# The last two batches of a latent attention: softmax sums taken on all 128 rows and inverted whole, in place of inverted on 32 rows and spread by DMA

## What is computed

```python
# latent attention: 16 heads, each batch has 64 context rows (masked) and 64 latent rows as keys
q  = layer_norm(x) @ Wq
kv = concatenate([layer_norm(ctx), layer_norm(x)], 1) @ Wkv
weight = softmax(where(mask, (q * scale) @ (k * scale).T, -max), axis=-1)   # over 128 keys
x = x + (weight @ v) @ Wout
# then: layer_norm(x); rmsnorm, quantise, @ w1, relu, square, rmsnorm, quantise, @ w2; + x; layer_norm
```

## Time and profile before

| | us |
|---|---|
| median of 3 runs | 1608.52 (1604.91 to 1608.94) |
| the profiled execution, its own time | 1607.23 |
| its span in the trace | 1605.4 |
| PE busy in the span | 1424.4 (89%) |
| DVE busy | 1134.2 (71%) |
| ACT busy | 963.8 (60%) |
| POOL busy | 303.9 (19%) |

### The profile page before, as it was taken

How to read it: one execution, slowest core, us unless ns; L and a number is a source line. 1 busy time by engine, 2 the same in 40 slices (tenths; PEclk the granted TensorE clock), 3 DMA queues, 4 the chain that set the end, 5 groups by cost and what they waited for, 6 DMA issues and landing times. The chain is left out here.

```text
span 1605.4 us, 32269 instructions
## 1 busy us (share of the span) xinstructions
PE 1424.4 (89%) x12643; PEld 868.5 (54%) x12658; DVE 1134.2 (71%) x2363; ACT 963.8 (60%) x1498; POOL 303.9 (19%) x278
## 2 busy tenths in 40 slices
PE   7999999998999788878887868999999999999962
PEld 4666666665664333334333345566666666666541
DVE  4666778885336799889988943445667767766788
ACT  2332367675555988789878944345556665555433
POOL 3434335352001100111010031111112211110101
PEclk9999999997999999999999979999999999999995
DMA  4000000001000000000000002222222222222210
GB/s 178 2 2 2 2 19 12 15 6 54 1 1 1 1 2 1 1 1 1 1 1 4 1 14 53 62 68 65 61 60 60 66 67 68 65 57 57 69 47 17
DMA packets 41013, 50.78 MB, mean 32 GB/s; under 512 B 9248, under 2 KB 23200, under 8 KB 40480
## 3 DMA queue, kind: packets, MB, share of 16 engines
q1 hardware_dynamic: 40576, 48.06, 11.7%
q10 hardware_dynamic: 288, 0.67, 0.1%
HBM read 13.04 MB, written 2.10 MB: 9 GB/s over the span
## 5 line engine op out<-in xcount | busy, mean ns | idle before, releaser
L1836 DVE TENSOR_TENSOR l_px<-psum,l_share 128x1024 f32<-128x1024 f32 x64 | 78.4, 1224 | 154.6 <-PE psum L1552 104.6
L1694 ACT ACTIVATE l_prob<-psum,l_bias 128x1024 f32<-128x1024 f32 x64 | 71.3, 1115 | 172.5 <-PE psum L1529 172.5
L1541 PE MATMUL psum<-l_XT,l_A 128*128 128x256 f32 x512 | 126.3, 391 | 3.3 <-ACT l_XT L1709 3.1
L1524 PE MATMUL psum<-l_th,l_XT 128*128 128x512 f32 x256 | 125.6, 613 | 1.4 <-DVE stream L1843 0.7
L1588 PE MATMUL psum<-l_px,l_N 128*128 128x256 f32 x512 | 124.2, 386 | 1.8 <-ACT l_r L1735 1.8
L1552 PE MATMUL psum<-l_prob,l_X 128*128 128x512 f32 x256 | 122.8, 603 | 0.0
L1817 DVE TENSOR_REDUCE l_top<-psum 128x8 bf16<-128x1024 f32 x64 | 78.2, 1221 | 43.6 <-PE psum L1603 43.5
L895 PE MATMUL psum<-f_projX,f_kT 64*128 64x512 f32 x256 | 77.1, 679 | 34.1 <-DVE f_frac L1266 18.6
L1588 PEld LDWEIGHTS psum<-l_px,l_N 128*128 128x128 f32 x512 | 94.0, 191 | 19.1 <-issue 4.7
L1541 PEld LDWEIGHTS psum<-l_XT,l_A 128*128 128x128 f32 x512 | 93.6, 193 | 15.0 <-ACT l_XT L1709 3.6
L1266 DVE TENSOR_TENSOR f_frac<-psum,f_whole 128x1024 f32<-128x1024 f32 x80 | 98.0, 1225 | 2.7
(11 more groups left out here) (309 smaller groups left out, 3198.9 us busy)
## 6 DMA issues: line engine op xcount, KB each, us to landing
l_share<-l_recip SPq DMA_DIRECT2D x512, 64.0 KB, 2.0
early_weights<-in_weights SPq DMA_DIRECT2D x1, 2405.0 KB, 11.2
c_cs<-in_ctx SPq DMA_DIRECT2D x16, 128.0 KB, 2.1
f_qf<-in_l_mats SPq DMA_DIRECT2D x1, 2048.0 KB, 8.0
out<-l_normed SPq DMA_DIRECT2D x16, 128.0 KB, 2.0
l_craw<-in_ctx SPq DMA_DIRECT2D x15, 128.0 KB, 2.3
late_weights<-in_weights SPq DMA_DIRECT2D x1, 1089.0 KB, 11.2
relbias<-in_relbias ACTq DMA_DIRECT2D x1, 512.0 KB, 5.2
```

What stands on the lines that cost most here:

```text
L1524: nc.tensor.matmul(ps[:, SC + n, :], XT[:, q % 3, k, :, :], th[:, q % 2, k, 8 * n:8 * n + 8, :], start=True, stop=False)
L1541: last = nc.tensor.matmul(ps[:, at + j // 2, (j % 2) * 256:(j % 2 + 1) * 256], A[:, QB * k + j, :], XT[:, q % 3, :, 1, :], start=True, sto ...
L1836: nc.vector.tensor_tensor(px[:, q % 2, :, k, :], ps[:, GA:GA + 2, :].rearrange("p a (h s) -> p (a h) s", s=S), share[:, (b // 2) % 2, b % ...
```

## The change

Only the last pair, p = 31 (batches 62 and 63), is treated otherwise.

- Its `sums`, `invert` and `spread` are gone: one `sums` (L1562 x8), two transposes and a small reciprocal, 16 DMAs.
- PE takes the sums of batch 62 (step 63) and 63 (step 64) with a 128 x 128 matrix of ones (`broad_sums`), so that the 1024 sums of a batch stand on all 128 rows in two banks: `RO` for 62, `SC` for 63.
- DVE inverts these 128 x 1024 sums whole, straight into `share` (`invert_last`): batch 62 at the end of step 63, batch 63 in step 64.
- `gather(63)` writes into `RO`, and waits for the first inversion (which reads `RO`) and no longer for the division of batch 62; it stands ahead of `tokens_turned(13)` now.
- On DVE `divide(62)` and `divide(63)` move to the front of steps 64 and 65, behind `tokens(13)` in step 64; `invert_last(63)` stands between `divide(62)` and `hidden_biggest(11)`. `hidden_turned` of jobs 11 and later on PE waits for the second inversion, which frees `SC`.

```diff
@@ SP
-                if i % 2 == 0 and 0 <= i - 2 < B:
+                if i % 2 == 0 and 0 <= i - 2 < B - 2:
                     spread((i - 2) // 2)
@@ PE, gather
-                if b >= 1:
+                at = GA
+                if b == B - 1:
+                    pe.wait_ge(s["last_share"], 1)
+                    at = RO
+                elif b >= 1:
                     pe.wait_ge(s["px_sb"], b)
                 for n in range(2):
-                    last = nc.tensor.matmul(ps[:, GA + n, :], X[:, q % 2, k, :], prob[:, b % 4, n, :], start=True, stop=True)
+                    last = nc.tensor.matmul(ps[:, at + n, :], X[:, q % 2, k, :], prob[:, b % 4, n, :], start=True, stop=True)
                 last.then_inc(s["px_ps"], 1)
+
+            def broad_sums(b):
+                pe.wait_ge(s["exped"], b + 1)
+                at = RO if b == B - 2 else SC
+                for n in range(2):
+                    last = nc.tensor.matmul(ps[:, at + n, :], ones32[:, :], prob[:, b % 4, n, :], start=True, stop=True)
+                last.then_inc(s["broad"], 1)
@@ PE, hidden_turned
+                if TQ * TQ * q + 21 >= B:
+                    pe.wait_ge(s["last_share"], 2)
@@ PE, the loop
+                if i - 2 == B - 1:
+                    gather(B - 1)
                 if job(i, 13) is not None:
-                    pairs = min(max(0, (i - 2) // 2 + 1), B // 2)
+                    pairs = min(max(0, (i - 2) // 2 + 1), B // 2 - 1)
                     pe.wait_ge(s["sums_read"], pairs)
                     tokens_turned(job(i, 13))
-                if 0 <= i - 2 < B:
+                if 0 <= i - 2 < B - 1:
                     gather(i - 2)
-                if i % 2 == 1 and 0 <= i < B:
+                if i >= B - 1 and i <= B:
+                    broad_sums(i - 1)
+                if i % 2 == 1 and 0 <= i < B - 2:
@@ DVE
+            def invert_last(b):
+                dve.wait_ge(s["broad"], b - B + 3)
+                dve.wait_ge(s["px_sb"], B - 4)
+                at = RO if b == B - 2 else SC
+                nc.vector.reciprocal(share[:, 1, b % 2, :, :], ps[:, at:at + 2, :]).then_inc(s["last_share"], 1)
@@ DVE, divide
-                dve.wait_ge(s[f"share{b % 2}{b // 2 % 2}"], 128 * (b // 4 + 1))
+                at = RO if b == B - 1 else GA
+                if b >= B - 2:
+                    dve.wait_ge(s["last_share"], b - B + 3)
+                else:
+                    dve.wait_ge(s[f"share{b % 2}{b // 2 % 2}"], 128 * (b // 4 + 1))
@@ DVE, the loop
                 if job(i, 12) is not None:
                     tokens(job(i, 12))
+                if i >= B and i <= B + 1:
+                    divide(i - 2)
+                if i == B:
+                    invert_last(B - 1)
                 if job(i, 20) is not None:
                     hidden_biggest(job(i, 20))
@@
-                if 0 <= i - 2 < B:
+                if 0 <= i - 2 < B - 2:
                     divide(i - 2)
-                if i % 2 == 1 and 0 <= i < B:
+                if i % 2 == 1 and 0 <= i < B - 2:
                     invert((i - 1) // 2)
+                if i == B - 1:
+                    invert_last(B - 2)
```

More of the change, by code:

```diff
@@ L1415, in latents_bitlinear_phase @@
         "px_ps px_sb y_ps yT_sb yt_ps out_read var1 root1 x_ready x_ps xiT_sb deq1 h_ps r_sb squared hh ss2 root2b hn q_ready q_ps hiT_sb "
-        "d_ps d_read var3 root3 normed stored0 stored1 steps asteps").split()}
+        "d_ps d_read var3 root3 normed stored0 stored1 steps asteps broad last_share").split()}
     w, ps = c["w"], c["psum"]
@@ L1671, in _ @@
                 if job(i, 22) is not None:
-                    pe.wait_ge(s["sums_read"], min(i // 2, B // 2))
+                    pe.wait_ge(s["sums_read"], min(i // 2, B // 2 - 1))
                     if job(i - 1, 13) is not None or job(i - 9, 13) is not None:
@@ L1832, in divide @@
                 dve.wait_ge(s["px_ps"], b + 1)
-                dve.wait_ge(s[f"share{b % 2}{b // 2 % 2}"], 128 * (b // 4 + 1))
+                at = RO if b == B - 1 else GA
[3 more added lines that the diff above has]
+                    dve.wait_ge(s[f"share{b % 2}{b // 2 % 2}"], 128 * (b // 4 + 1))
                 if k == 0 and q >= 2:
                     dve.wait_ge(s["y_ps"], q - 1)
-                nc.vector.tensor_tensor(px[:, q % 2, :, k, :], ps[:, GA:GA + 2, :].rearrange("p a (h s) -> p (a h) s", s=S),
+                nc.vector.tensor_tensor(px[:, q % 2, :, k, :], ps[:, at:at + 2, :].rearrange("p a (h s) -> p (a h) s", s=S),
                                         share[:, (b // 2) % 2, b % 2, :, :].rearrange("p a (h s) -> p (a h) s", s=S),
```

## The result

| | before | changed |
|---|---|---|
| median of 6 runs each, us | 1606.99 (1603.36 to 1609.52) | 1617.99 (1613.11 to 1619.28) |
| span of the profiled execution | 1605.4 | 1616.4 |

The ratio is 1.0068, 95% interval 1.0049 to 1.0086: 11.0 us slower, where 9.0 had been summed and 1617 us forecast. Six runs of the changed kernel on another occasion gave 1.0078 (1.0061 to 1.0094).

What follows compares the result with a forecast made beforehand. DVE's program order was taken to bound the kernel from step 63; 6.12 us removed, two 6.55 us inversions and later terms put residual(14) 9.0 us later, giving 1617 us (0.5% slower), range 1612.7 to 1620.

Steps and rivals of the forecast that it cites:

- What bounds: From step 63 on DVE's program order sets the end; PE is no longer the busiest engine there.
- What goes: On DVE: 1.67 us of transposes and small reciprocal, 3.61 us DMA wait, 0.84 us wait for gather(63); together 6.12 us.
- The price: Each whole 128x1024 reciprocal on DVE costs 6.55 us, from a line through five short reciprocals.
- broad_sums: On PE, broad_sums(62) ends 0.88 us later than the old sums(31), so the first inversion starts at 1533.47.
- DVE's order: DVE's pieces summed from the first inversion at 1533.47 to the end of hidden_quantised(11)'s last wide piece at 1556.44.
- The turn to residual(14): From hidden_quantised(11)'s last wide piece via PE and ACT to residual(14): 4.80 us, as one job later, reaching 1561.24.
- bound of the whole turn at the low clock: Upper case for the turn before residual(14): combine 3.8 us in place of 3.10, about 1562.1, 9.9 us later than before.
- The tail gives nothing back: After residual(14) DVE is the path until the end and everything behind shifts; at most 1.2 us returns in job 12's turn.
- eight passes: Rival on the inversions: eight pipe turns an element, 8.7 us each, the pair 4.3 us more, 1621 us; 3%.
- partly cheaper long form: Rival on the inversions: long reciprocals cost say 4 us each, 5.1 us less than the sum, 1612 us; 3%.
- cheap reciprocal: Rival on both inversions: 1.22 us each like the maxima, PE becomes the bound, 1.2 us earlier than before, 1607 us; 5%.
- with PE warm: In the cheap reciprocal rival: normalise(10) ends 3.63 us after DVE's hi piece, at 1551.0, with no low-clock delay from PE.

Runs made afterwards that it cites:

- e1: Changed kernel with its two whole reciprocals replaced by plain copies of the same sums, leaving out that division: 1603.81 us, ratio to before 0.9986.
- e2: Changed kernel with each of the two whole reciprocals done twice in a row on DVE: 1631.26 us, ratio to before 1.0151.
- e3: Changed kernel with eleven useless matmuls in PE's pause, eight before tokens_turned(13) and three after it: 1612.68 us, ratio to before 1.004.
- e4: Kernel before with only gather(63) moved into RO ahead of tokens_turned(13): 1605.6 us, ratio to before 0.9998.
- v1: Against before: small inversion kept, PE spreads its result, ACT copies it to share; gather(63) into RO, divide(63) earlier: 1605.68 us, ratio 0.9994.
- v2: v1 with gather(62) and the spreading right behind hidden(12), plus useless matmuls in four PE pauses: 1598.4 us, ratio to before 0.9972.

## Why the prediction was right, point by point

- **What bounds**: right. From step 63 on the time follows DVE's order nearly one to one: 10.65 us more on DVE cost 10.31 (e1), 13.1 cost 13.06 (e2). What comes on top is DVE's wait for PE at the low clock.
- **What goes**, 6.12 us: right. All three pieces are gone in the trace after, and no DMA moves in its first window (share 0.00).
- **The price**, 6.55 us by a line through five short reciprocals: right to 0.01 us (6.56 and 6.55). The step from 32 elements to 1024 was the boldest of the sum and its largest term. The size of it was well founded, the closeness is in part luck. Neighbouring rows of the five give slopes from 5.0 to 7.5 ns an element, which is 5.3 to 7.8 us for 1024, and the trace of before had two more rows that were not used, both of 28 elements, where the line says 328 ns:

```profile
L1309 DVE RECIPROCAL l_rstd<-l_rstd x1: 329/329/329, 930.2 to 930.2; 128x28 f32<-128x28 f32 x1
...
L1296 DVE RECIPROCAL rstd<-rstd x1: 270/270/270, 928.1 to 928.1; 128x28 f32<-128x28 f32 x1
```

One lies on the line and one 58 ns under it. The estimate of 1.22 us from the Trainium skill ("VectorE: DVE Perf Modes", "Side-by-side: where the cycles go for N=2048 bf16", one element a cycle for everything) does not hold for this instruction: measured are (6.552 - 0.153) / 1024 = 6.25 ns an element. The repeat count of 8 in the section "First, the fixed hardware budget" of that page of the Trainium skill, read as eight cycles an element, is an estimate of 8.7 us; the measurement lies under that as well.

- **broad_sums**, 0.88 us: a little too dear. The first inversion started 1.72 us after divide(61), where the transpose had started 1.14 after it, so 0.58. The term compared the ends of PE's work, but before the change DVE had not been waiting for PE at this place: the old sums ended at 1531.34 + 1.06 = 1532.40, and DVE was busy with divide(61) until the transpose at 1532.59. That slack of 0.2 us took up part of the 0.88.
- **DVE's order**: forecast 24.99 us from divide(61) to the end of hidden_quantised's last wide piece (1556.44 - 1531.45), measured 1556.39 - 1531.90 = 24.49. Half a microsecond less, of which 0.3 is the point above.
- **The turn to residual(14)**, 4.80 us: too cheap, and the one term whose reasoning was inconsistent. 5.68 were measured (1562.07 - 1556.39), near the bound of the whole turn at the low clock. The text says that this turn will begin at the 1.2 GHz level, and then takes the price of job 12's turn. That one had begun at the high clock and fell on the way, as its hidden_turned shows:

```profile
1563.13 0.62 PE L1624 MATMUL psum<-ident,l_hi 128*128 128x128 bf16 x8 [2.48 <-DVE l_hi L1867]
```

In the changed kernel, after 9.94 and 3.61 us of pause, the same eight matmuls took 1.01 us and combine 3.72, where the bound had said 3.8. e3 shows the clock to be the cause.

- **The tail gives nothing back**: right in the main (e2), but it took something more. residual(15) waited 2.06 us in place of 1.18, and the piece up to it is 1.03 us longer. I had listed that turn only as one that might get cheaper. It did not: that turn ran at the low clock from its start in both traces of the changed kernel, and in e2 and e3 too (hidden_turned 1.01 us, combine 3.72 to 3.73). In before, e1, e4 and v1, the kernels without a whole reciprocal or filling, it began at the high clock (0.61 to 0.62 us). Why the clock fell earlier there, on the same work with other pauses, is open. It does not take a low clock throughout the turn before, for in e3 that one's hidden_turned and combine ran at the high clock.
- **Sum**: 9.0 forecast, 10.55 in the trace from divide(61): less 0.5 for DVE, plus 0.9 for the turn, plus 1.0 and 0.1 for the tail. The other 0.45 us of the difference of the spans lie ahead of divide(61), where PE happened to be slower (scores(63) took 2.99 us and not 1.98). That 1617 met 1617.99 within 1 us is luck: the forecast started from a median of 1608.52, and six runs gave 1606.99, while the difference was 11.0 us and not 9.0. The 9.0 lie within the interval of the ratio, 7.9 to 13.8 us.
- **The rivals**: eight passes and a partly cheaper long form are out by the 6.55 us. The cheap reciprocal was run as e1: I had given it 1.2 us under before; from divide(61) on it is 0.24 us over, and the medians, 1.9 us under, do not tell either from no change. The step that failed there is "with PE warm": the turn ran at the low clock again (combine 3.19 us, and a wait of 1.53 us at residual(14)). So even a reciprocal at the price of a copy would have made this change worth nothing in the trace.

## What to carry to other kernels

Price an instruction by the slope of its own kind at several sizes, not by another operation of the same size: a reciprocal that costs 178 ns on four columns costs 6.55 us on 1024, and the transposes and DMAs that looked like a detour keep it to 16 columns. Before a wait is traded for work, put the two sums side by side on the engine that sets the order: here 6.1 us of waits and small pieces against 13.1 us of work. And when TensorE's pause grows, price its next work at the low clock: here 3.72 us in place of 1.95.

## What the runs showed of the hardware

- A VectorE reciprocal of float32 took some 0.153 us and 6.25 ns for each element of a row: 178 ns for 4, 353 for 32, 6.55 us for 1024. Nothing between 32 and 1024 was measured. With PSUM as the source it lay on the same line (16 and 1024 elements). Maximum, copy and product over the same 128x1024 from PSUM took 1.22 to 1.23 us.
- Four float32 products of 32 rows by 128x512, on four row groups and into four banks, took 1.14 us together, where two of 128 rows took 1.88. Spreading 32-row pieces over 128 rows on PE and copying them on ACT (1.94 us for two batches) replaced 16 DMAs whose first eight took 6.3 us from the first issue at 1534.36 to the last landing at 1538.71 + 1.98 = 1540.69.
- Work without use in TensorE's pause had its clock at the high level when the real work came: with filling the same eight matmuls took 1.95 us in place of 3.72 (e3, and so in v2). It does not hold the clock by itself: after a gap of 2.35 us in e3 it fell to 0.57 for the next stretch. Filling that starts at the low level runs long: four pieces took 5.62 us in v2, where three took 2.79 at the high level, and in e3 such filling held up the real work a little.
